# Attention head outputs brought into channel order through HBM instead of by TensorE transposes

## The reference

```python
# layer 0: 8 heads of 8 channels, keys only within 64 positions of the query
scores = einsum('bqhd,bkhd->bhqk', q, k) / sqrt(8)
scores = where(abs(i - j) <= 64, scores, -max)
o = einsum('bhqk,bkhd->bqhd', softmax(scores), v).reshape(n, t, e)
o = transpose(o @ w_out.T + b_out, (0, 2, 1))
x = x + einsum('nit,io->not', relu(o) * ctx, w_ct) + b_ct
# layer 1: rotary embedding on q and k (k and v from ctx), no band, no gate
out = softmax(q k / sqrt(8)) v            # back to [b, 64, 256]
x = x + einsum('oc,bct->bot', Wo, out) + bo
```

## Time and profile before

| | us |
|---|---|
| median of 3 runs (range) | 1429.04 (1427.28 to 1431.03) |
| span of the profiled execution | 1429.4 |
| PE busy in the span | 1315.2 (92%) |
| DVE, ACT, POOL busy | 955.8, 874.6, 716.5 |
| layer 0 attention, steady part | 110 to 590, one iteration 15.89 |
| feed-forward 1 and its start-up | 600 to 690 |
| layer 1 attention, steady part | 700 to 1170, one iteration 15.22 |
| feed-forward 2 | 1195 to 1429 |

### The profile page before, as it was taken

The page is one execution under the profiler, slowest core; times in us unless marked ns, Lnnn a source line. Parts: engine busy times, 40 slices in busy tenths (PEclk is TensorE's granted clock), DMA queues, the critical chain, the costliest instruction groups (busy, mean ns, idle before and its releaser), DMA issues.

```text
span 1429.4 us, 37785 instructions
## 1 busy us (share of the span) xinstructions
PE 1315.2 (92%) x11332; PEld 910.0 (64%) x11332; DVE 955.8 (67%) x2156; ACT 874.6 (61%) x1909; POOL 716.5 (50%) x1292
## 2 busy tenths in 40 slices
PE   1999999999999998882799999999999989999998
PEld 1666777777777776571466666666666655766675
DVE  6438878787888787468888888888888872111110
ACT  1147676666666667563488888888888875122211
POOL 6336777777777776404555655656656511010000
PEclk9869999999999999995799999999999999999999
DMA  8314444444344443001434444444444410000000
GB/s 243 78 36 95 103 100 90 96 100 100 90 96 100 100 90 87 6 12 37 92 91 104 105 95 103 103 97 104 102 97 107 93 41 1 15 30 15 15 15 29
DMA packets 90797, 111.18 MB, mean 78 GB/s; under 512 B 15056, under 2 KB 82384, under 8 KB 83056
## 3 DMA queue, kind: packets, MB, share of 16 engines
q1 hardware_dynamic: 83184, 103.38, 31.9%
q10 hardware_dynamic: 7552, 7.02, 1.7%
HBM read 16.52 MB, written 4.19 MB: 14 GB/s over the span
## 4 chain that ended last, share of the span: by engine, by line
PE 62%; POOL 11%; issue 11%; DVE 8%; ACT 2%; ACTq 1%; DMA 1%; POOLq 1%; SPq 1%; DVEq 1%
PE bank L459 10%; PE bank L420 8%; PE bank L652 8%; PE bank L643 8%; PE bank L436 7%; PE bank L418 5%; PE bank L470 4%; DVE row_max L1031 3%; PE bank L501 3%; POOL rot L1216 2%; PE bank L614 2%; POOL Qp L1205 2%; PE bank L490 1%; POOL k_rest L1221 1%; POOL q_rest L1201 1%
## 5 line engine op out<-in xcount | busy, mean ns | idle before, releaser
L1031 DVE TENSOR_REDUCE row_max<-bank 128x2 f32<-128x384 f32 (+1 forms) x1024 | 599.6, 617 | 148.5 <-PE bank L420 146.8
L687 ACT ACTIVATE probs<-bank 128x384 f32<-128x384 f32 (+1 forms) x1024 | 534.4, 542 | 161.8 <-PE bank L436 155.0
L420 PE MATMUL bank<-Ks,Qs 96*128 96x192 bf16 (+1 forms) x2048 | 372.1, 264 | 13.5 <-DMA Ks<-Ks 8.4
L436 PE MATMUL bank<-Qs,Ks 128*128 128x192 bf16 (+1 forms) x2048 | 367.1, 261 | 13.6 <-ACT probs L687 12.5
L1234 POOL TENSOR_SCALAR_AFFINE_SELECT probs<-probs 128x256 f32<-128x256 f32 (+1 forms) x512 | 257.2, 526 | 175.1 <-ACT probs L687 156.3
L420 PEld LDWEIGHTS bank<-Ks,Qs 96*128 96x128 bf16 x2048 | 189.3, 99 | 122.8 <-issue 37.8
L459 PE MATMUL bank<-probs,V 128*32 128x192 f32 (+1 forms) x4096 | 249.0, 361 | 3.7 <-POOL probs L1234 2.4
L436 PEld LDWEIGHTS bank<-Qs,Ks 128*128 128x128 bf16 x2048 | 188.9, 98 | 40.1 <-ACT probs L687 23.9
L418 PE MATMUL bank<-band,ident 128*128 128x384 bf16 x512 | 169.2, 331 | 1.0 <-ACT out_bias L840 0.5
L459 PEld LDWEIGHTS bank<-probs,V 128*32 128x32 f32 x4096 | 107.4, 109 | 82.7 <-issue 41.8
L1171 DVE TENSOR_TENSOR X<-bank,X 128x256 f32 (+1 forms) x32 | 13.6, 425 | 184.6 <-PE bank L652 184.6
(11 more groups left out here) (128 smaller groups left out, 1776.9 us busy)
## 6 DMA issues: line engine op xcount, KB each, us to landing
Ks<-Ks SPq DMA_DIRECT2D x64, 576.0 KB
Qs<-Qs SPq DMA_DIRECT2D x128, 192.0 KB
Qs<-Qp SPq DMA_DIRECT2D x192, 64.0 KB
Ks<-Kp SPq DMA_DIRECT2D x192, 64.0 KB
side<-in_ctx SPq DMA_DIRECT2D x64, 128.0 KB, 2.0
X<-in_x ACTq DMA_DIRECT2D x4, 1024.0 KB, 10.4
out<-X SPq DMA_DIRECT2D x8, 512.0 KB, 2.9
Qs<-max_rows SPq DMA_DIRECT2D x128, 12.0 KB
```

Source lines behind the costliest of these rows:

```text
L420: last = nc.tensor.matmul(dst[:, blk * win:(blk + 1) * win], Qs[0:SHIFT_ROW, pair[1], h, blk * P:(blk + 1) * P], Ks[0:SHIFT_ROW, pair[1], ...
L436: last = nc.tensor.matmul(dst[:, blk * win:(blk + 1) * win], Ks[:, pair[1], h, blk * P:(blk + 1) * P], Qs[:, pair[1], h, start(blk):start( ...
L687: nc.scalar.activation(probs[:, h % 8, 0:2 * win], exp_bank[h % 2][:, 0:2 * win], ACT.Exp, scale=SCALE).then_inc(s["exped"], 1)
L1031: nc.vector.tensor_reduce(row_max[:, pair[1], h, :], bank_of(pair, h)[:, 0:2 * win].rearrange("p (b k) -> p b k", b=2), AX.X, ALU.max).the ...
```

## The change

The sums and the head outputs are no longer transposed on PE. After the second `heads_out` of a pair SP writes all of `heads_sb` (128 partitions x 4 KB) to a DRAM tensor `spill` (`spill_heads`), waits for its landing, and reads two 128 x 256 tensors back in channel order (`gather_heads`, rows of 1 KB): the outputs into `normed`, and the sums into `sums`. For that the ones column of V becomes eight columns, so that each sum is there once per channel. `normalise` becomes one reciprocal over 128 x 256 and one multiply in place over 128 x 256, both SBUF to SBUF, once per pair at h = 14 for pair m1. `turn_heads`, `turn_back` and `back_out` are gone; the output projection takes `normed` directly. It, `relu`, `gate`, `mix` and `update` now work on pair `m2` = r-2, at the same steps as before. The jobs heads0, heads1 and back leave the bank orders. The weights of the output projection and the value bias are permuted to the new channel order on the host side, as q and k already were. The tails hold the rest of two pairs.

```diff
 JOBS = {
-    "A": [("q", AHEAD), ("heads1", -1), ("v", 2), ("max0", 1), ("heads0", 0)],
-    "B": [("max1", 0), ("k", AHEAD), ("back", -1), ("out", -1), ("mix", -1)],
+    "A": [("q", AHEAD), ("v", 2), ("max0", 1)],
+    "B": [("max1", 0), ("k", AHEAD), ("out", -2), ("mix", -2)],
 }
-FIRST_FULL, LAST_FULL = 1, PAIRS - 1 - AHEAD
+FIRST_FULL, LAST_FULL = 2, PAIRS - 1 - AHEAD
...
         heads_sb = sb("heads_sb", [P, 2, 2 * T])
-        rcp = sb("rcp", [P, 2, HPP])
-        normed = sb("normed", [P, RING, 2, P])
-        mixed_in = sb("mixed_in", [P, T])
+        normed = sb("normed", [P, RING, T])
+        sums = sb("sums", [P, T])
+        spill = nc.dram_tensor("spill", (P, 4 * T), fp32)
...
         TAIL = ((PAIRS - 1) // RING, (PAIRS - 1) % RING)
+        TAIL2 = ((PAIRS - 2) // RING, (PAIRS - 2) % RING)
...
+            def spill_heads(pair):
+
+                if not active(pair):
+                    return
+                wait_apart(e, (s["heads_out"], num(pair) * 2 + 2), (s["gathered"], num(pair) * 32))
+                e.dma_start(spill[:, :], heads_sb[:, :, :].rearrange("p a t -> p (a t)")).then_inc(s["spilled"], 16)
+
+            def gather_heads(pair):
+
+                if not active(pair):
+                    return
+                wait_apart(e, (s["spilled"], (num(pair) + 1) * 16), (s["normed"], num(pair)),
+                           job_wait(s, l, "B", "out", at(pair, -RING), "filled"))
+                for dst, row in ((normed[:, pair[1], :], 0), (sums[:, :], HD)):
+                    e.dma_start(dst, bass.AP(spill[:, :].tensor, row * 4 * T, [[T, HD * 4], [32 * 4 * T, 4], [1, T]])
+                                ).then_inc(s["gathered"], 16)
+
             def iteration(r):
                 load_side(at(r, AHEAD + 1 if l else 0))
                 lay_out(at(r, 2))
                 shift_rows(r, 1)
+                spill_heads(at(r, -1))
                 replicate(at(r, 2))
+                gather_heads(at(r, -1))
                 shift_rows(at(r, 1), 0)
 
...
-            def turn_heads(pair, half):
-
-                if not active(pair):
-                    return
-                wait_bank(e, s, l, "A", f"heads{half}", pair)
-                e.wait_ge(s["heads_out"], num(pair) * 2 + half + 1)
-                for blk in range(2):
-                    for g in range(2):
-                        last = nc.tensor.transpose(job_bank["A"][:, (blk * 2 + g) * P:(blk * 2 + g + 1) * P],
-                                                   heads_sb[:, half, g * T + blk * P:g * T + (blk + 1) * P],
-                                                   ident[:, :])
-                last.then_inc(s["A_filled"], 1)
-
-            def turn_back(pair):
-                if not active(pair):
-                    return
-                wait_bank(e, s, l, "B", "back", pair)
-                wait_job(e, s, l, "A", "heads1", pair, "read")
-                for blk in range(2):
-                    last = nc.tensor.transpose(job_bank["B"][:, blk * P:(blk + 1) * P],
-                                               normed[:, pair[1], blk, :], ident[:, :])
-                last.then_inc(s["B_filled"], 1)
-
-            tail = {0: lambda: values_group(TAIL, 3), 2: lambda: turn_heads(TAIL, 1), 4: lambda: turn_back(TAIL),
-                    5: lambda: project("B", "out", TAIL, WO, mixed_in[:, :],
-                                       lambda: wait_job(e, s, l, "B", "back", TAIL, "read"))}
+            def project_out(pair):
+                if not active(pair):
+                    return
+                project("B", "out", pair, WO, normed[:, pair[1], :],
+                        lambda: e.wait_ge(s["normed"], num(pair) + 1))
...
             if l == 0:
-                tail[8] = lambda: project("B", "mix", TAIL, 4, gated, lambda: e.wait_ge(s["gated"], PAIRS))
+                tail = {0: lambda: values_group(TAIL, 3), 2: lambda: project_out(TAIL2),
+                        4: lambda: project("B", "mix", TAIL2, 4, gated, lambda: e.wait_ge(s["gated"], PAIRS - 1)),
+                        8: lambda: project_out(TAIL),
+                        10: lambda: project("B", "mix", TAIL, 4, gated, lambda: e.wait_ge(s["gated"], PAIRS))}
+            else:
+                tail = {0: lambda: values_group(TAIL, 3), 1: lambda: project_out(TAIL2),
+                        6: lambda: project_out(TAIL)}
...
-                    if h == 5:
-                        turn_heads(m1, 1)
-                    if h == 8:
-                        turn_back(m1)
                     if h == 8:
                         project_v(p2)
                     if h == 10:
-                        project("B", "out", m1, WO, mixed_in[:, :],
-                                lambda: wait_job(e, s, l, "B", "back", m1, "read"))
+                        project_out(m2)
                     if h == 12:
                         turn_max("A", p1, 0)
                     if h == 14 and l == 0:
-                        project("B", "mix", m1, 4, gated,
-                                lambda: e.wait_ge(s["gated"], num(m1) + 1))
-                    if h == 14:
-                        turn_heads(r, 0)
+                        project("B", "mix", m2, 4, gated,
+                                lambda: e.wait_ge(s["gated"], num(m2) + 1))
...
                 e.wait_ge(s["pv_done"], num(pair) * 4 + 2 * half + 2)
-                wait_job(e, s, l, "A", f"heads{half}", at(pair, -1), "filled")
+                wait_some(e, s["spilled"], num(pair) * 16)
...
-            def back_out(pair):
-                if not active(pair):
-                    return
-                wait_job(e, s, l, "B", "back", pair, "filled")
-                nc.scalar.activation(mixed_in[:, :], job_bank["B"][:, 0:T], ACT.Copy).then_inc(s["B_read"], 1)
...
-            tail = {1: lambda: heads_out(TAIL, 1), 4: lambda: back_out(TAIL)}
+            tail = {1: lambda: heads_out(TAIL, 1)}
             if l == 0:
-                tail[6] = lambda: relu(TAIL)
+                tail[3] = lambda: relu(TAIL2)
+                tail[9] = lambda: relu(TAIL)
...
-                    if h == 8:
-                        back_out(m1)
...
                     if h == 10 and l == 0:
-                        relu(m1)
+                        relu(m2)
...
-            def normalise(pair, half):
-
-                if not active(pair):
-                    return
-                wait_job(e, s, l, "A", f"heads{half}", pair, "filled")
-                turned = job_bank["A"][:, :].rearrange("p (n c) -> p n c", c=32)
-                nc.vector.reciprocal(rcp[:, half, :], turned[:, :, HD]).then_inc(s["rcp_done"], 1)
-                e.wait_ge(s["rcp_done"], num(pair) * 2 + half + 1)
-                wait_job(e, s, l, "B", "back", at(pair, -RING), "filled")
-                nc.vector.tensor_tensor(
-                    normed[:, pair[1], :, half * CH:(half + 1) * CH].rearrange("p b (h d) -> p b h d", d=HD),
-                    turned[:, :, 0:HD].rearrange("p (b h) d -> p b h d", b=2),
-                    rcp[:, half, :].rearrange("p (b h) -> p b h", b=2).unsqueeze(3)
-                    .broadcast_to([P, 2, HEADS, HD]),
-                    ALU.mult).then_inc(s["A_read"], 1)
+            def normalise(pair):
+
+                if not active(pair):
+                    return
+                e.wait_ge(s["gathered"], (num(pair) + 1) * 32)
+                nc.vector.reciprocal(sums[:, :], sums[:, :]).then_inc(s["rcp_done"], 1)
+                e.wait_ge(s["rcp_done"], num(pair) + 1)
+                heads = normed[:, pair[1], :]
+                nc.vector.tensor_tensor(heads, heads, sums[:, :], ALU.mult).then_inc(s["normed"], 1)
...
-            tail = {3: lambda: normalise(TAIL, 1), 8: lambda: update(TAIL)}
+            tail = {5: lambda: update(TAIL2), 7: lambda: normalise(TAIL), 11: lambda: update(TAIL)}
 
             def iteration(r):
-                p1, p3, m1 = at(r, 1), at(r, AHEAD), at(r, -1)
+                p1, p3, m1, m2 = at(r, 1), at(r, AHEAD), at(r, -1), at(r, -2)
                 for h in range(HPP):
-                    if h == 5:
-                        normalise(m1, 1)
                     if h == 6:
                         apply(at(r, AHEAD + 1))
                     if h == (14, 10)[l]:
-                        update(m1)
+                        update(m2)
                     if h == 14:
-                        normalise(r, 0)
+                        normalise(m1)
...
-                    gate(m1)
+                    gate(m2)
                     mask_group(r, 2)
...
+            if l == 0:
+                gate(TAIL)
...
-            nc.gpsimd.memset(V[:, :, :, :, HD:HD + 1], 1.0).then_inc(cleared_q, 1)
+            nc.gpsimd.memset(V[:, :, :, :, HD:2 * HD], 1.0).then_inc(cleared_q, 1)
```

(12 more changed lines are left out.)

24 lines of the change are left out of this document (10 added, 14 removed).

## The result

| | before, us | after, us |
|---|---|---|
| median (range) | 1429.88 (1427.28 to 1431.03) | 1508.26 (1503.43 to 1509.85) |
| span of the profiled execution | 1429.4 | 1506.8 |
| PE busy | 1315.2 | 1287.1 |
| DVE busy | 955.8 | 1016.5 |

The changed kernel is slower: 1.0549 times the time before, 95% interval 1.0524 to 1.0575, 78 us. The forecast of 1486 us is 22 us short of it, and the range of 1445 to 1540 us holds it. PE has less to do, as meant, and waits more.

The account below looks back on a forecast made before the run. DVE's written order and the DRAM round trip were taken to close the loops, making iterations 1.05 us (layer 0) and 0.9 us (layer 1) longer: 29 x (1.05 + 0.9) = 57 us on 1429.4, 1486 us; range 1445 to 1540 us.

Parts of the forecast that it names:

- The bound and the place: Layer 0: DVE owns the section from mix to the next turn_max, so longer normalise at h = 14 lengthens it, 5.29 to 6.92 us.
- The reciprocal: In normalise on DVE: 256 elements per partition take 1.75 us, by the slope of 6.25 ns per further element.
- DVE alone: Rival: only DVE's serial work counts, the round trip is hidden; iterations 0.92 and 0.4 us longer, 1467 us; chance 0.18.
- The round trip: Heads through DRAM and back before normalise: gathers land 11.7 us after turn_max in layer 0; loops of 16.87 and 16.0 us.
- The term that fails: SP's queue between spill and gathers: replicate moves its 960 KB in 5.2 us, back to back.
- 0.1 of margin: Layer 1: added because the 15.6 us loop is only 0.4 us shorter and now and then the later; 16.0 taken as 16.1.
- DVE's last leg: Layer 0: from the maximum behind normalise to the next turn_max, kept at the earlier kernel's 331.53 - 328.56.
- outside these iterations: Ends beyond 29 iterations per layer: r = 31 and the feed-forward tails set against each other at nothing, +-3 us.
- later round trip: Rival: the round trip sets both loops, with slower gathers and replicate; priced at 1536 us; chance 0.19.
- The bound of 74 us: PE work removed, two turn_heads and one turn_back per pair, over both layers: the gain if PE bound every section.
- What the profile was to show: Signs if right: reciprocal some 1.75 us, PE waiting at h = 1 and 3 in layer 0, iterations of 16.9 and 16.1 us.

Follow-up runs that it names:

- the kernel with the spare reciprocal: Kernel before, plus one 128 x 256 reciprocal on DVE behind the normalise of h = 14, read by nobody: 1478.27 us, ratio 1.0344.
- the transfers alone: Kernel before, plus the spill and two gathers into tiles nobody reads: 1431.74 us, ratio 1.0017.
- the kernel with (4, 7): Changed kernel, normalise in two 128-column halves on the pair before last, at h = 4 and 7 (layer 0), 2 and 5 (layer 1): 1410.29 us.

## Why the prediction was right, and where it was off

*The bound and the place.* Right: the section from `mix` to the next `turn_max` in layer 0 belongs to DVE, and what lengthens `normalise` at h = 14 lengthens it. Measured in the iteration from 317.01 to 333.76: 10.01 us to `mix` (at 327.02) and 6.74 behind it, where 9.89 and 6.92 were computed. The second is near by two misses that cancel, named below.

*The reciprocal.* Right in size: 1751 ns against 1754 from the slope over 8 and 32 elements. That slope was the step on which the sign hung, and the run without the reciprocal shows the sign turning with it. The multiply took 0.42 us in the row above, as computed, but 0.50 on average in layer 0, and 0.65 in the kernel without the round trip. The Trainium skill, VectorE: DVE Perf Modes, section First, the fixed hardware budget, whose repeat count of eight had given an estimate of 2.13 us, is not borne out by this row in size.

*DVE alone.* Computed 16.81 and 15.6 us, measured without the round trip 16.53 and 15.56. In layer 0 the term was 0.3 too large. The way from the maximum behind `normalise` to `turn_max` was taken as the 2.97 us of before, and is 333.76 - 331.32 = 2.44 in the changed kernel, 0.53 less. Of that 0.41 is again the first instruction of `split_max`, 0.57 us before:

```profile
332.71 0.16 DVE L925 TENSOR_SCALAR max_parts<-row_max 128x16 bf16<-128x16 f32 x1
```

In the kernel with the spare reciprocal this way was 0.58 shorter, and that is why the 328.19 - 326.53 = 1.66 us to the next maximum cost 1.07.

*The round trip.* This is the step that was mis-sized. The end of `heads_out` in both layers (ACT):

```profile
318.70 0.60 ACT L730 ACTIVATE heads_sb<-bank 128x512 f32<-128x512 f32 x1 [0.33 <-PE bank L477]
...
906.05 0.58 ACT L730 ACTIVATE heads_sb<-bank 128x512 f32<-128x512 f32 x1
```

From there to the start of the reciprocal, 9.35 us were computed for layer 0 and 9.7 for layer 1. Measured: 329.19 - 319.30 = 9.9 and 917.08 - 906.63 = 10.45. The term that fails is `replicate`, taken as 5.2 us of data when its issues follow back to back. In the packets of the trace (8 KB each) its data end 8.6 us after `heads_out` in layer 0 and 9.0 in layer 1, on average, where 7.8 and some 8.15 were computed; the spill's end at 2.5 and 2.95, near the 2.6 and 2.95 computed. From the end of the spill's data to there the queue is no fuller than the 0.74 of the earlier trace rows:

```profile
321.80:327.90 6.10, 6.10 (x68) 4.58 (x61) 4.68 (x13) 4.30 (x10) 5.85 (x11) 1.00 0.73 177
```

The gathers behind it were sized rightly: they land at 9.7 and 10.2, 1.1 to 1.2 us after the last of `replicate`, where 1.4 was computed. Their 5.4 us from issue to landing are thus mostly the queue ahead of them, which the forecast had in it.

In layer 1 the round trip sets the pace, and its excess is the miss: 10.45 + (903.14 - 900.27) + (906.63 - 903.14) = 16.81 us in this iteration and 16.62 on average, where 9.7 + 2.83 + 3.48 = 16.0 and 0.1 of margin were computed. In layer 0 the agreement is luck. The round trip was 0.54 too short in the sum and DVE's last leg 0.53 too long, so that the loop came to 16.75 us in the iteration shown against 16.87; the ordinary iterations last 16.6, under the forecast of 16.95, and those at the lower clock bring the mean to 17.04. In all it is 29 x (0.09 + 0.52) = 18 us, and with 77.4 - 74 = 3 us outside these iterations, taken as nothing in the forecast, that is the miss of 22 us. The rival "later round trip" had the right mechanism, a slower `replicate`, and too high a price. Its 1536 us also do not follow from its terms: half of 1.5 us is 0.75 in each loop, not 1.0 and 0.8, which gives some 1528.

*The clock.* Not in the prediction: 4 of the 16 iterations in layer 0 lost 1.7 us each at the lower level of the clock, 0.4 us per iteration on average, and one in layer 1, with the same fall, lasted 18.0 us. It went with the late gathers and the reciprocal at h = 14 together: the kernels without a round trip, with the gathers ahead of Ks, and without the reciprocal show no such iterations.

*What the removed PE work is worth.* The bound of 74 us was not used in the sum, rightly: with only the multiply in its place it gave 42. In layer 1 the iteration went from 15.22 to 15.01 only, with PE then waiting 0.65 us for POOL's `split_max`.

*What the profile was to show.* PE's waits at h = 1 and 3 in layer 0 were announced as some 2 us, and are 0.99 + 0.68. DVE's wait ended by a DMA was expected in layer 1 and short or none in layer 0: 0.91 to 1.15, and 0.34. Not seen: PE waiting at h = 0 for the stack or for `shift_rows`, in line with the transfers alone costing 0.2%.

## What to carry to other kernels

Work that leaves a full engine must be weighed against the duration and the place of what replaces it on an engine with written order: one reciprocal of 1.74 us, put where PE waited for what stands behind it, cost 49 us, and the changed kernel's work cut in two and put elsewhere let the change gain 1.4%. Price an instruction never seen at its size from the slope over its own sizes, not from other operations of that shape. And where an engine waits for a result that is read back from memory, the read should be issued ahead of bulk copies in its queue: that order alone was worth 47 us.

## What was not expected of the hardware

An issue on SP's queue can itself take long: the second gather's took 2.55 us behind the 576 KB copy and 0.59 us ahead of it, for the same 128 KB.

PE's granted clock fell to 0.52 for 3.4 us right after an iteration's waits of 0.99 and 0.68 us, after 12.70 us in which it had been busy 10.72. The iteration before it had waits of 1.08 and 0.68 us at the same two steps, and its clock stayed at 1.00, so the size of these two waits does not tell which iterations fall.

Of DVE's small instructions, several took two sizes: the half multiply 0.29 or 0.69 us, `xn` 0.40 or 0.84, the first instruction of `split_max` 0.16 or 0.57, the same forms. In the kernel with (4, 7) the longer multiply of layer 0 runs beside POOL, and ends as POOL's next instruction starts:

```profile
320.50 0.69 DVE L1054 TENSOR_TENSOR normed<-normed,sums 128x128 f32<-128x128 f32 x1
...
319.46 1.59 POOL L1218 TENSOR_SCALAR_AFFINE_SELECT probs<-probs 128x256 f32<-128x256 f32 x3 [1.91 <-ACT probs L684]
321.21 0.41 POOL L1218 TENSOR_SCALAR_AFFINE_SELECT probs<-probs 128x256 f32<-128x256 f32 x1 [0.16 <-POOL probs L1218]
```

The Trainium skill, SBUF — State Buffer, section SBUF: two separate sides, says that a VectorE instruction with two SBUF inputs and a GpSimd instruction exclude each other for a whole instruction. The 0.69 us row agrees in kind: it is 0.40 us longer than the 0.29 of the other half, and one of POOL's three merged selects beside it takes some 0.53. No run here took POOL's work away to show it.
